# Where the float32r operands lie in SBUF: one contiguous region, and eight weight places at eight residues of 128 bytes

## The reference

```python
def _L0_attn_ref(x, ...):            # D_MODEL 256, D_HIDDEN 512, B 4, L 1024
    x = silu(depthwise_conv(x @ w1.T))           # 3 taps
    x_delta = softplus(x @ dl_w.T + dl_b)
    A_bar = exp(-x_delta * (x @ A_w.T + A_b))
    B_x = x @ B_w.T + B_b
    h = cumsum(B_x * cumprod(A_bar, axis=1), axis=1)
    ssm_out = h @ C_w.T + C_b + x @ D_w.T + D_b
    z = ssm_out * silu(ssm_out @ w2.T)
    return ssm_out + z @ w3.T

def _L0_ffn_ref(x, ...):             # E 8 experts, F 1024, K 2 per token, shared expert of 256
    xn = layernorm(x) * gamma + beta
    topv, topi = top_k(softmax(xn @ router_w), 2); topv = topv / sum(topv)
    out = sum over e of comb[:, e] * (silu(clip(gate_e)) * up_e) @ down_w[e]
    return out + the same with the shared expert's weights

x = x + layernorm(attn(layernorm(x)))
x = x + layernorm(ffn(layernorm(x)))
```

## The kernel before

| tensor | byte | modulo 128 |
|---|---|---|
| w_both | 24128 | 64 |
| xs_hi, xs_lo | 93888, 102080 | 64 |
| h_hi[0], h_hi[1] | 126720, 134912 | 0 |
| h_lo[0], h_lo[1] | 143104, 151296 | 0 |
| ring places 0 to 5 | 24128 + 6144 f | 64 |
| ring places 6, 7 | 93888, 102080 | 64 |

## Time and profile before

### The profile page before, as it was taken

One profiled execution on the slowest core, in us unless ns is written; L12 is line 12 of the kernel. 1 busy time (PEld: TensorE's weight loads), 2 busy tenths in 40 slices (PEclk: granted clock), 3 DMA queues, 4 the chain that ended last, 5 costly groups with the idle time before them and its releaser, 6 DMA issues.

```text
span 1187.3 us, 23315 instructions
## 1 busy us (share of the span) xinstructions
PE 1096.2 (92%) x7492; PEld 973.6 (82%) x7492; DVE 833.9 (70%) x2113; ACT 654.8 (55%) x1325; POOL 302.9 (26%) x358
## 2 busy tenths in 40 slices
PE   3989999899979989999999999999999999999940
PEld 2765776677757656999999999999999999999940
DVE  5986899898888667666666666666666666666645
ACT  6768867778584354444444444445444444444425
POOL 1142033723441624121221122122112211221225
PEclk9999999999999999999999999999999999999975
DMA  8654766973665779532231245555922356211239
GB/s 304 220 194 173 248 231 211 316 237 142 221 232 168 249 260 344 158 67 58 54 71 18 36 130 194 189 172 184 370 34 36 85 199 230 36 28 25 36 87 214
DMA packets 96617, 191.70 MB, mean 161 GB/s; under 512 B 8768, under 2 KB 59456, under 8 KB 96576
## 3 DMA queue, kind: packets, MB, share of 16 engines
q1 hardware_dynamic: 80160, 170.38, 41.9%
q0 software_dynamic: 16416, 20.85, 10.2%
HBM read 295.62 MB, written 86.41 MB: 322 GB/s over the span
## 4 chain that ended last, share of the span: by engine, by line
PE 80%; DVE 7%; issue 3%; DMA 3%; ACT 2%; POOL 2%; SPq 1%; another core or an unknown queue 0%; DVEq 0%; ACTq 0%; POOLq 0%
PE bank L1336 12%; PE bank L1335 12%; PE bank L1337 12%; PE bank L462 11%; PE bank L1346 6%; PE bank L1348 6%; PE bank L1347 6%; PE bank L456 4%; PE bank L458 4%; PE bank L457 4%; PE bank L1323 1%; DVE xr L1476 1%; POOL xs_scratch L1142 1%; DVE a_cum L867 1%; SPq L441 1%
## 5 line engine op out<-in xcount | busy, mean ns | idle before, releaser
L1335 PE MATMUL bank<-h_hi,w_both 128*128 128x256 f32 x936 | 268.2, 287 | 0.2 <-DVE cv L1452 0.2
L1445 DVE TENSOR_SCALAR cv<-bank 128x256 f32<-128x256 f32 x312 | 132.3, 424 | 193.1 <-PE bank L1337 193.1
L1285 POOL DMA_INDIRECT acc_scratch<-cv,ids x78 | 126.1, 1616 | 554.3 <-DVE cv L1424 513.6
L1337 PE MATMUL bank<-h_hi,w_both 128*128 128x256 f32 x936 | 261.2, 279 | 0.0
L1336 PE MATMUL bank<-h_hi,w_both 128*128 128x256 f32 x936 | 261.2, 279 | 0.0
L1395 ACT ACTIVATE cv<-cv 128x256 f32<-128x256 f32 x312 | 130.3, 418 | 233.8 <-DVE cv L1445 233.0
L1387 ACT ACTIVATE h_hi<-cv 128x256 fp32r<-128x256 f32 x312 | 129.8, 416 | 115.0 <-DVE cv L1452 115.0
L1335 PEld LDWEIGHTS bank<-h_hi,w_both 128*128 128x128 f32 x936 | 177.4, 190 | 0.4 <-issue 0.4
L1336 PEld LDWEIGHTS bank<-h_hi,w_both 128*128 128x128 f32 x936 | 176.1, 188 | 0.0
L1337 PEld LDWEIGHTS bank<-h_hi,w_both 128*128 128x128 f32 x936 | 175.7, 188 | 0.0
L1452 DVE TENSOR_TENSOR cv<-bank,cv 128x256 f32<-128x256 f32 x312 | 132.6, 425 | 47.4 <-ACT cv L1395 34.6
(11 more groups left out here) (227 smaller groups left out, 2391.5 us busy)
## 6 DMA issues: line engine op xcount, KB each, us to landing
w_both<-w_split SPq DMA_DIRECT2D x228, 768.0 KB
xs_hi<-w_split SPq DMA_DIRECT2D x38, 768.0 KB
xs_lo<-w_split SPq DMA_DIRECT2D x38, 768.0 KB
e_raw<-w_e SPq DMA_DIRECT2D x64, 384.0 KB
w_split<-e_high SPq DMA_DIRECT2D x64, 384.0 KB
w_split<-e_raw SPq DMA_DIRECT2D x64, 384.0 KB
u<-xs_scratch SPq DMA_DIRECT2D x40, 260.0 KB
x_in<-x SPq DMA_DIRECT2D x8, 512.0 KB
```

The source lines that it names most:

```text
L1335: nc.tensor.matmul(out, e_hi[f][:, cols], xg_hi[:, par, c, :], start=c == 0, stop=False)
L1337: i = nc.tensor.matmul(out, e_lo[f][:, cols], xg_hi[:, par, c, :], start=False, stop=c == DC - 1)
L1445: nc.vector.tensor_scalar(gate[:, f % 4, :], gu_ps[f % 2][:, 0:G], CLIP, -CLIP, ALU.min, ALU.max).then_inc(clipped, 1)
```

## The change

The declarations are put in another order, and the places of the ring are chosen anew. The five kinds of float32r tensors now follow each other directly, from byte 24128 on: `w_both`, `xs_hi`, `xs_lo`, `h_hi`, `h_lo`; the float32 tensors that stood between them come later, and `w_full` and `ones` at the very end. The ring's eight places are now: places 0 to 3 at the four quarters of `w_both` (9216 bytes apart), 4 and 5 in `xs_hi` and `xs_lo`, 6 and 7 in `h_lo[0]` and `h_lo[1]`; and place f begins f x LINE = 4 f floats, 16 f bytes, behind the start of its home.

```diff
+LINE = 4
...
         w_both = sb("w_both", [P, 2 * W_COLS], F32R)
-        w_full = sb("w_full", [P, F_COLS])
-        ones = sb("ones", [P, HALF])
+        xs_hi = sb("xs_hi", [P, DC, L], F32R)
+        xs_lo = sb("xs_lo", [P, DC, L], F32R)
+        h_hi = [sb(f"h_hi{i}", [P, HC, HALF], F32R) for i in range(2)]
+        h_lo = [sb(f"h_lo{i}", [P, HC, HALF], F32R) for i in range(2)]
         x_in = sb("x_in", [P, LT, D])
...
-        ring = [w_both[:, f * 2 * CW:(f + 1) * 2 * CW] for f in range(FC - 2)] + [flat(v[:, :, :])[:, 0:2 * CW] for v in (xs_hi, xs_lo)]
+        quarter = W_COLS // 2
+        ring_homes = [w_both[:, f * quarter:(f + 1) * quarter] for f in range(4)] + [flat(v[:, :, :]) for v in (xs_hi, xs_lo, h_lo[0], h_lo[1])]
+        ring = [home[:, f * LINE:f * LINE + 2 * CW] for f, home in enumerate(ring_homes)]
```

More of the change, by code:

```diff
@@ L76, in mixer @@
         cv = sb("cv", [P, DC, L])
-        linear = sb("linear", [P, 1])
-        xs_hi = sb("xs_hi", [P, DC, L], F32R)
-        xs_lo = sb("xs_lo", [P, DC, L], F32R)
         delta = sb("delta", [P, 2, HALF])
@@ L86, in mixer @@
         carry_h = sb("carry_h", [P, HC])
-        h_hi = [sb(f"h_hi{i}", [P, HC, HALF], F32R) for i in range(2)]
-        h_lo = [sb(f"h_lo{i}", [P, HC, HALF], F32R) for i in range(2)]
         s = sb("s", [P, DC, HALF])
@@ L96, in mixer @@
         knee = sb("knee", [P, HC])
+        linear = sb("linear", [P, 1])
         st = sb("st", [P, LT, 6])
@@ L126, in mixer @@
         e_high = sb("e_high", [P, WS, CW])
+        w_full = sb("w_full", [P, F_COLS])
+        ones = sb("ones", [P, HALF])
         w_hi, w_lo = w_both[:, 0:W_COLS], w_both[:, W_COLS:2 * W_COLS]
```

## The result

The changed kernel takes 1194.62 us (median of 4 runs, 1191.97 to 1198.47); the kernel before takes 1184.32 us beside it (4 runs, 1182.9 to 1186.98). The ratio is 1.0096, with a 95% interval of 1.0066 to 1.0126: it is slower, and the forecast of 1176 us missed even the sign. That the time lies inside the wide range of the prediction, 1166 to 1195 us, by 0.4 us, says nothing for the forecast: the range took in most of the rivals. In a second series of 12 runs against 23 of the kernel before the ratio was 1.0047 (1.0029 to 1.0064), slower too, but by less than the 0.5% from which the prediction counts a change. The profiled execution takes 1191.97 us, its span is 1189.9 us. (The profiled execution of before, 1189.42 us, was slower than all four of its other runs, and that of the changed kernel the fastest of its four, so the two spans hide most of the difference.)

What follows compares the result with a forecast made beforehand. TensorE's matmul spacing in the gapless expert loop was taken as the bound. Expert products gave -6.9 us, all other terms 0: 1183.3 - 7 = 1176 us for the median; forecast's own range 1165 to 1178, wide range 1166 to 1195 us.

Steps and rivals of the forecast that it cites:

- What bounds the kernel: Expert loop, 488.70 to 1141.78 us: TensorE has no gap at full clock, so only the spacing of matmuls counts.
- The two levels and the distance: Expert products take 113.3 or 117.8 ns; both levels are stable at distance 64, and a seam can throw between them.
- a place with different levels in successive rounds: Expert loop: sign that the prediction's reasons are wrong, whatever the time; no size given.
- Part (1): Expert products: seams into `gate_up` get 64 instead of 0, short share rises from 0.31 to about 0.6, gaining 6.9 us.
- The upper bound of part (1): Expert products: if all spacings were as bad as the worst found behind a seam, 120 ns, a loss of 17 us.
- Part (2): First half's 512-column products: distance of `h_hi`, `h_lo` to `w_both` goes from 64 to 0; 0 us, ends -2 and +2.
- Part (3): Weight DMAs to 16-byte steps: 0 us, with 2.0 us to spare at the double change; 10% slower packets cost about +2 us.
- Rival C: Weight DMAs: writes at 16-byte steps are slower and the double change of expert comes too late; 1189 us, chance 0.07.
- Part (4): Places of `x_in`, `u`, `cv`, `w_full` for float32 matmuls, VectorE and ScalarE: 0 us, ends -1 and +1.
- Rival A: Expert products: levels come from order and moment of a run's start, not distance; 1183 us, same, chance 0.30.
- Rival B: Expert loop seams: changing distances leave hardly any short run and add transients; 1191 us, chance 0.22.
- Rival D: Expert products: all spacings short, the most part (1) allows; 1165 us, counted as the forecast's far end, no separate chance.

Runs made afterwards that it cites:

- second kernel of experiment 5: Changed kernel, all ring places 64 bytes behind their homes' starts, with a 128-byte gap before `h_hi[1]`: 34.44 us a round, 1183.81 us beside 1180.3.
- Experiments 2 and 3: Changed kernel with old ring: 35.40 us a round; kernel before with new ring: 35.16; changed kernel, all places at distance 32: 34.90, or 96: 35.08.
- experiment 1: Changed kernel with every ring place at distance 64 instead of staggered: 34.40 us a round; timed later, 1179.83 us, ratio to before 0.9953.
- experiment 5: Four changed kernels with places at 64, some mixed with 192, two with a 128-byte gap before `h_hi[1]`: rounds of 34.72, 34.44, 34.65 and 34.52 us.
- experiment 4: Changed kernel with all ring places at distance 192 instead of staggered: 34.41 us a round, 1177.08 us beside 1180.3.

## Why the prediction was wrong

**What bounds the kernel** held. The stretch is full of matmuls before and after, the clock is 1.00, and only the spacing moved the time.

**The two levels and the distance** held in part. Distances do decide: 34.40 us a round at 64, 35.40 at 0. Behind the first round every place has the same level in all rounds of the kernel before and of the changed one, and the short level never came below 113 ns. But the prediction named a place with different levels in successive rounds as a sign that its reasons are wrong, and the second kernel of experiment 5 has such places: the level is not a matter of distances and seams alone.

**Part (1), the step that failed: "of 8 seams into `gate_up` in a turn, those that now throw a short run into a long one lose their cause", and from it a short share of 0.31 to 0.6 and -6.9 us.** It took the distance within the runs for harmless. I had written that for 16, 32, 48, 80, 96 and 112 the trace has no example, and then chose a value near the middle of the bounds as if only the seams mattered. The share went from 0.31 to 0.07 (20 of 288), and the loop lost 10 us. Experiments 2 and 3 show the reason: at 0, 32 and 96 there is no short level, whatever the seams do. Seven of eight chunks had left the one distance (64 modulo 128) at which runs of 113 ns were on record. (16, 48, 80 and 112 were seen only between chunks of other distances. The eighth, chunk 4, kept 64 and was long too; why is not shown.) And the seam itself was misread: experiment 1, with distance 0 at both seams and 64 in all runs, has more short products (114) than before. Where the loss lies can be added up from the starts in the two traces. Of the 0.54 us a round, 0.46 are inside the runs, from the third spacing on; the first two spacings behind each seam together give 0.01, the seams themselves 0.06, the transposes the rest.

**The upper bound of part (1)** was right in size, by luck. All at 120 ns was priced at +17 us; the kernel with distance 0 everywhere costs 0.91 x 19 = 17.3 us in the loop. But the price was taken from two spacings of the earlier trace rows that lie inside `down`, at distance 64 modulo 128, and show nothing of distance 0. The mean after is (17.52 - 0.9) / 140 = 118.7 ns against 116.8, which is 1.9 ns x 140 x 37.9 = 10 us.

**Part (2), the first half at 0 us with ends of -2 and +2,** was too narrow: -3.4 us. I compared at distance 0 and 64 modulo 128 and found 0.5 ns. Modulo 256 those were distances of 128 and 64; after the change all are 0 modulo 256, and these products run at 226.7 ns, in groups with `xs` (where modulo 128 nothing changed) as in those with `h`. What fits this is a period of 256 bytes or more; for the products with `h` the gap of experiment 5 shows it, 231 ns at distances of 128 in part against 227 at 0. It is also another order than in the loop: distance 0 is the best of those seen for 512 columns and the worst for 256. Why is open.

The rule of the Trainium skill that a weight load takes no read bandwidth from the running matmul (TensorE: Matmul & The Clock Gate, section "Step-by-step: what each phase is for") would, as I read it, have every one of these kernels at one round time. The runs decide otherwise: 34.40 to 35.40 us with the same instructions. Whether the two reads really meet, and in which unit, no run shows.

**Part (3), the weight DMAs at 0 us,** held to 0.3 us, but its slack was read at the wrong place. The double load of the earlier trace rows after, the first matmul that reads the last place behind it, which answers to the earlier trace rows, and the gap of the one longer round:

```profile
819.78:858.17 38.39, 38.33 (x324) 38.10 (x323) 24.41 (x69) 17.45 (x43) 8.32 (x6) 1.00 0.98 355
```

```profile
860.31 0.28 PE L1338 MATMUL bank<-h_hi,h_lo 128*128 128x256 f32 x1
```

```profile
848.89 0.38 PE L1326 MATMUL bank<-ident,u 128*128 128x128 f32 x2
...
849.32 0.19 PEld L1338 LDWEIGHTS bank<-h_hi,w_both 128*128 128x128 f32 x1 [0.29 <-issue]
849.33 0.38 PE L1338 MATMUL bank<-h_hi,w_both 128*128 128x256 f32 x1
```

38.39 us instead of 37.60, 355 GB/s instead of 363, and the last place is read 2.1 us behind the end of the window, as before (2.0). Part of this may be the slower turn, which frees the places later. But neither the window's end nor the last place tells the slack. The trace holds when each chunk landed, and place 2 of the second load is the tightest: before, it landed at 850.91 us and was first read at 851.10, 0.19 us later; after, it landed at 849.21, and the weights of the first matmul that reads it began to load at 849.32. TensorE stands still for 0.3 us ahead of that `gate_up`, and this is the gap of the one longer round. (The kernel of experiment 4 has the same: 839.46 and 839.58 us.) So the double load was on the edge already before, and a DMA slower by 10% would have come some 2.8 us late at place 2 (estimate: a tenth of the 28.6 us from 822.30 to that landing, less 0.1), not 1.8 at the last place.
Rival C is right in where a wait would show, and out as the cause of the 10 us: the wait is 0.3 us, in one profile of the changed kernel and not in the other. The loads themselves are hardly slower: places 2 to 7 land 1.88 us apart after and 1.87 before.
By the rule of the Trainium skill on transfers off a 256-byte boundary (DMA: Bandwidth & Descriptors, section "How a descriptor splits into AXI transactions") the old places were off it as well, so little should change; the rates, 363 and 355 GB/s, agree.

**Part (4)** at 0 stands untested by itself; the sums above leave between 1 us less and 3 us more for it and for everything else that was not counted.

**Rival A** (the levels come from the moment, not from the distance) is out as a forecast, by the rounds of experiments 1 to 3: the distance moves the time. Half of its reason stands, by the alternating chunk of experiment 5: at one distance and the same addresses a run can have either level.

**Rival B** gave 1191 us and came nearest. Its condition, under a fifth of the spacings short, was met, and its first term, all long, 5.3 us, is about half of what was lost: from the third spacing of each run on, 117.8 ns everywhere instead of the mean before is 0.31 us a round. Its second term, transients behind seams, is not what the other half is: the first two spacings behind the seams cost 0.01 us a round more than before. Most of the rest is levels above the long one, 0.15 us a round: 118.9 to 119.5 ns on average in the chunks at distances 0, 80, 96 and 112. That its sum of 1191 us came near is in part luck. **Rival D** (all short, 1165 us) was never reached; the best layout has 114 of 288 short.

**Open:** what the levels are and why seams flip them; whether the places 6 and 7 of the kernel before, which lie at 192 modulo 256 from the tokens while the others lie at 64, are what sets it 0.09 us a round behind experiment 1; the exact period of the pattern; whether a layout exists in which all runs are short (at most 18.5 us, by the bound of part (1)); and why the loop starts up to 16 us earlier or later from one execution to the next.

## What to carry to other kernels

Where TensorE runs without a gap and the work is many short products, the byte position of the moving operand against the next stationary one is worth up to 3% of such a stretch. Read the spacing by operand in the timeline, look for the residues at which it is shortest, and give all operands that distance, rather than spreading them evenly. Do it for each width by itself: here 512 columns were fastest at distance 0, where 256 were slowest. A value for which the trace has no example is no neutral value: when a change leaves the one distance that is on record as good, reckon with a loss. And read the slack of a row of DMAs place by place, from landing to first use; the last one need not be the tightest.

## What the runs showed of the hardware

Products of 256 columns with float32r operands, at the full clock: 113.3 or 117.8 ns each at a distance of 64 or 192 bytes modulo 256, with the level flipping at certain seams and in most runs stable between them; 120.0 ns at 0; a wandering spacing with a mean of 118.2 and 118.9 ns in the kernels with 32 and 96. For 512 columns the mean was 232.5 ns in the old and 228.4 ns in the new arrangement, and for those with `h` 227 ns at distance 0 and 231 ns with part of them at 128. I had not expected that a level, once entered, mostly holds over a whole chunk and is the same in round after round, that in one kernel a chunk takes both levels in turn from round to round, nor that two layouts equal modulo 128 bytes differ by 0.32 us in a round.
